# One fused attention and mixture kernel: the three row buffers become a ring of twelve 512-column pieces

## The reference

```python
h = _layernorm(x) * (1 + ca) + sa
q, k, v = linear(h) ; scores = q @ k.T / sqrt(128)
qp = linear(h, Wtq)                     # two coordinates per token
diff = qp[i] - qp[j]
dist_sq = sum(diff ** 2)
forward_bias = 0.5 * (1 + cos(atan2(diff_y, diff_x)))
valid = (dist_sq <= mean + 1.25 * std) & causal
weights = softmax(where(valid * forward_bias == 0, -inf, scores))
x = x + ga * (h + linear(weights @ v) + 0.1 * linear(qp / norm(qp)))
h = _layernorm(x) * (1 + cb) + sb
x = x + gb * mixture(h)   # top 4 of 16 experts by routing, and 2 shared ones
```

## Time and profile before

| what | us |
|---|---|
| median of 3 runs | 665.44 |
| lowest and highest | 664.79, 666.22 |
| the profiled execution, its own time | 664.28 |
| span of the profiled execution | 662.5 |
| TensorE busy | 568.8 |
| VectorE busy | 512.1 |
| ScalarE busy | 362.5 |
| GpSimd busy | 362.1 |

### The profile page before, as it was taken

One profiled execution on the slowest core, in us unless ns is written; L12 is line 12 of the kernel. 1 busy time (PEld: TensorE's weight loads), 2 busy tenths in 40 slices (PEclk: granted clock), 3 DMA queues, 4 the chain that ended last, 5 costly groups with the idle time before them and its releaser, 6 DMA issues.

```text
span 662.5 us, 10953 instructions
## 1 busy us (share of the span) xinstructions
PE 568.8 (86%) x3524; PEld 342.4 (52%) x3524; DVE 512.1 (77%) x1448; ACT 362.5 (55%) x722; POOL 362.1 (55%) x325
## 2 busy tenths in 40 slices
PE   2846878887877899898989999799988599999995
PEld 1734445565653454354545555465554365656563
DVE  3588899997776688656776675756976999898887
ACT  0623567687642633356775868655455355555552
POOL 4459455844104452869977677733314355555553
PEclk9997679898987799899998999999999999999999
DMA  6501000000004121131112220122100000000000
GB/s 187 159 2 35 1 0 1 1 0 1 1 13 115 69 72 45 63 96 49 63 48 60 69 65 32 51 63 63 49 1 16 2 1 17 2 17 2 17 1 17
DMA packets 21840, 26.01 MB, mean 39 GB/s; under 512 B 2628, under 2 KB 11864, under 8 KB 21784
## 3 DMA queue, kind: packets, MB, share of 16 engines
q1 hardware_dynamic: 21784, 25.33, 13.1%
HBM read 23.09 MB, written 2.23 MB: 38 GB/s over the span
## 4 chain that ended last, share of the span: by engine, by line
PE 42%; DVE 34%; issue 8%; ACT 7%; POOL 6%; SPq 1%; DMA 1%; DVEq 0%; ACTq 0%; POOLq 0%
PE bank L805 7%; PE bank L1053 7%; PE bank L806 7%; PE bank L807 6%; DVE row L1322 4%; PE bank L954 4%; DVE stage L1536 4%; ACT stage L745 4%; DVE pen L1328 3%; DVE row L1333 3%; DVE ysb L1515 2%; PE bank L939 2%; POOL sw L580 2%; PE bank L844 2%; PE bank L914 2%
## 5 line engine op out<-in xcount | busy, mean ns | idle before, releaser
L594 POOL TENSOR_TENSOR gp<-stage,gp 128x512 f16<-128x512 f32 x72 | 83.6, 1161 | 73.6 <-ACT gp L762 73.6
L580 POOL TENSOR_TENSOR sw<-hid,gp 128x512 f32<-128x512 f32 x64 | 81.4, 1271 | 76.9 <-DVE hid L1462 70.4
L1462 DVE SCALAR_TENSOR_TENSOR hid<-stage,bank 128x512 f32<-128x512 f32 x72 | 49.2, 684 | 63.5 <-ACT stage L745 62.1
L745 ACT ACTIVATE stage<-bank 128x512 f32<-128x512 f32 x144 | 84.7, 588 | 22.9 <-PE bank L807 22.6
L762 ACT CAST gp<-stage 128x512 f16<-128x512 f32 x72 | 44.4, 617 | 72.8 <-DVE stage L1536 72.8
L538 POOL TENSOR_TENSOR row<-row,dx 128x512 f32<-128x512 f32 (+3 forms) x48 | 54.6, 1141 | 54.3 <-ACT dx L642 54.0
L699 ACT COPY ptr<-bank 128x512 f32<-128x512 f32 (+2 forms) x80 | 41.5, 518 | 78.2 <-PE bank L939 77.6
L1053 PE MATMUL bank<-stage,wd 128*128 128x512 f32 x144 | 76.7, 615 | 7.2 <-DVE ysb L1467 7.2
L954 PE MATMUL bank<-v,ptr 128*128 128x128 f32 x544 | 77.0, 283 | 3.3 <-DVE x L1308 3.3
L954 PEld LDWEIGHTS bank<-v,ptr 128*128 128x128 f32 x544 | 70.9, 200 | 5.3 <-issue 3.9
L1515 DVE SCALAR_TENSOR_TENSOR ysb<-bank,comb,ysb 128x128 f32<-128x128 f32 x240 | 67.1, 342 | 0.1
(11 more groups left out here) (256 smaller groups left out, 1315.9 us busy)
## 6 DMA issues: line engine op xcount, KB each, us to landing
gp<-shares SPq DMA_DIRECT2D x64, 256.0 KB, 3.1
out_x<-x SPq DMA_DIRECT2D x8, 256.0 KB, 2.3
stage<-in_L_ffn_gate_w SPq DMA_DIRECT2D x1, 576.0 KB, 7.5
stage<-in_L_ffn_up_w SPq DMA_DIRECT2D x1, 576.0 KB, 4.2
stage<-in_L_ffn_gate_w SPq DMA_DIRECT2D x1, 448.0 KB, 6.9
stage<-in_L_ffn_up_w SPq DMA_DIRECT2D x1, 448.0 KB, 3.6
row<-in_L_wmod SPq DMA_DIRECT2D x1, 384.0 KB
stage<-in_L_ffn_sh_gate_w SPq DMA_DIRECT2D x1, 128.0 KB, 5.6
```

The costliest lines, as they stand in the source:

```text
L580: pool.tensor_tensor(sw[:, s % 2, :], hid[:, s % 2, :], wb[:, n % HELD_WEIGHTS, :], ALU.mult)\
L594: pool.tensor_tensor(gp[:, n % HELD, 1, :], act_g[:, s % 2, :], gp[:, n % HELD, 0, :], ALU.subtract)\
L745: act.activation(sg[:, s % 2, :], gate_bank(s)[:, :], func, scale=half_of / (H_UP * W_UP))\
```

## The change

`row` keeps its size but is now read as a ring of 12 pieces of 512 columns; chunk m lies in piece m % 12. The table `MEASURES_AT` is gone. In every slot n, ScalarE makes the rise of chunk n + 6, and GpSimd its measure where GpSimd has that chunk. In input piece 24, ahead of slot 0, six chunks are made in place of two. The wait of a rise is now for the turning of chunk m - 12. Masking, exponential and transposes address the new place; their sizes and counts are the same.

```diff
-ROWS = 3
+UNITS = 12
+AHEAD = 6
...
-RISE_AT = {CHUNKS_BEFORE[i - ROWS + 1] + CHUNKS_ROW[i - ROWS]: i for i in range(ROWS, BLK)}
-
-MEASURES_AT = {0: [2]}
-for slot, i in RISE_AT.items():
-    for c in range(CHUNKS_ROW[i]):
-        MEASURES_AT.setdefault(slot + c, []).append(CHUNKS_BEFORE[i] + c)
...
+        def unit_of(m):
+
+            k, o = divmod(m % UNITS, CH)
+            return row[:, k, o * W:(o + 1) * W]
...
@@ gpsimd, input piece 24 and the slots
                 if k == PIECES - 1 and b:
-                    for m in range(2):
+                    for m in range(AHEAD):
                         measure(b, m)
...
-                for m in MEASURES_AT.get(n, ()):
-                    if by_pool(b, m):
-                        measure(b, m)
+                if n + AHEAD < NCH and by_pool(b, n + AHEAD):
+                    measure(b, n + AHEAD)
...
@@ scalar, rise
-                if i >= ROWS:
-
-                    act.wait_ge(probs_turned, NCH * b + CHUNKS_BEFORE[i - ROWS] + min(c + 1, CHUNKS_ROW[i - ROWS]))
-                act.activation(row[:, i % ROWS, lot], yb[:, lot], ACT.Abs, bias=nyi[:, i:i + 1]).then_inc(rise_ready, 1)
+                if m >= UNITS:
+
+                    act.wait_ge(probs_turned, NCH * b + m - UNITS + 1)
+                act.activation(unit_of(m)[:, 0:w], yb[:, lot], ACT.Abs, bias=nyi[:, i:i + 1]).then_inc(rise_ready, 1)
...
@@ scalar, input piece 24 and the slots
-                    for m in range(2):
+                    for m in range(AHEAD):
                         rise(b, m)
...
-                for m in MEASURES_AT.get(n, ()):
-                    rise(b, m)
+                if n + AHEAD < NCH:
+                    rise(b, n + AHEAD)
```

More of the change, by code:

```diff
@@ L181, in build @@
         pen = sb("pen", [P, 2, W], BF16); dx = sb("dx", [P, 2, W])
-        row = sb("row", [P, ROWS, N])
+        row = sb("row", [P, 3, N])
         gsgn, gmag, graw = (row[:, 0, k * W:(k + 1) * W] for k in range(3))
@@ L536, in measure @@
                 pool.wait_ge(dx_ready, pooled(b, m))
-                o = row[:, i % ROWS, c * W:c * W + w]
+                o = unit_of(m)[:, 0:w]
                 pool.tensor_tensor(o, o, dx[:, pooled(b, m) % 2, 0:w], ALU.subtract).then_inc(measure_ready, 1)
@@ L702, in attention @@
                     i, c = CHUNKS[m]
-                    lot = slice(c * W, min((c + 1) * W, (i + 1) * P))
+                    probs = unit_of(m)[:, 0:min(W, (i + 1) * P - c * W)]
                     act.wait_ge(max_ready, BLK * b + i + 1)
-                    act.activation(row[:, i % ROWS, lot], row[:, i % ROWS, lot], ACT.Exp, bias=nmx[:, i:i + 1],
+                    act.activation(probs, probs, ACT.Exp, bias=nmx[:, i:i + 1],
                                    accum_out=rsum[:, i, c:c + 1]).then_inc(probs_ready, 1)
-                for m in MEASURES_AT.get(n, ()):
-                    rise(b, m)
+                if n + AHEAD < NCH:
+                    rise(b, n + AHEAD)
                 if n in NORM_AT:
@@ L939, in attention @@
                         last = pe.transpose(ring(b, 2, m)[:, k * P:(k + 1) * P],
-                                            row[:, i % ROWS, j * P:(j + 1) * P], ident[:, :])
+                                            unit_of(m)[:, k * P:(k + 1) * P], ident[:, :])
                     last.then_inc(probs_turned, 1)
@@ L1314, in attention @@
                     L = (i + 1) * P
-                    o = row[:, i % ROWS, :]
+                    w = min(W, L - c * W)
+                    o = unit_of(n)
                     if by_pool(b, n):
@@ L1321, in attention @@
                         dve.wait_ge(rise_ready, NCH * b + n + 1)
-                        step(dve.scalar_tensor_tensor(out=o[:, lot], in0=xb[:, lot], scalar=nxi[:, i:i + 1],
-                                                      in1=o[:, lot], op0=ALU.add, op1=ALU.subtract, reverse1=True))
+                        step(dve.scalar_tensor_tensor(out=o[:, 0:w], in0=xb[:, lot], scalar=nxi[:, i:i + 1],
+                                                      in1=o[:, 0:w], op0=ALU.add, op1=ALU.subtract, reverse1=True))
                         settle()
-                    w = min(W, L - c * W)
                     dve.wait_ge(dist_made, NCH * b + n + 1)
                     dve.scalar_tensor_tensor(out=pen[:, n % 2, 0:w], in0=ring(b, 1, n)[:, 0:w], scalar=0.0,
-                                             in1=o[:, c * W:c * W + w], op0=ALU.min, op1=ALU.min)\
+                                             in1=o[:, 0:w], op0=ALU.min, op1=ALU.min)\
                        .then_inc(dist_used, 1)
@@ L1332, in attention @@
                     dve.wait_ge(scores_made, NCH * b + n + 1)
-                    dve.tensor_tensor_reduce(o[:, c * W:c * W + w], ring(b, 0, n)[:, 0:w], pen[:, n % 2, 0:w],
+                    dve.tensor_tensor_reduce(o[:, 0:w], ring(b, 0, n)[:, 0:w], pen[:, n % 2, 0:w],
                                              float(P) ** -0.5 / QK_UP ** 2, -3.0e38, ALU.add, ALU.max,
```

## The result

The changed kernel takes 669.09 us (median of 16 runs, 667.17 to 672.61), the kernel before 666.15 in 16 runs beside it (664.38 to 668.24). The ratio is 1.005, with a 95% interval of 1.0036 to 1.0064: 3.3 us slower by the ratio, while the two medians are 2.9 apart. The profiled execution took 668.51 us with a span of 666.7, 4.2 more than the 662.5 of before. 6.0 us were predicted.

The account below looks back on a forecast made before the run. Bound by VectorE in batch 0; in batch 1 by ScalarE's chain at step 25, then GpSimd, then TensorE. 4.9 + 1.1 - 0.8 + 0.8 = +6.0 us on the median 665.44 gives 671.4, range 668.4 to 673.8.

Parts of the forecast that it names:

- The new wait: In every slot, a rise of chunk m waits for the turning of chunk m - 12; claimed to add 0.
- Six pairs ahead of step 25: Batch 1, input piece 24: ScalarE does chunks 2 to 5 before step 25's activation, on the path; +4.9 us (4.4 to 5.3).
- GpSimd's stretch: Batch 1, from step 25's `weigh` to the layer norm's power: heavier measures on gapless GpSimd; +1.1 us (0 to 1.5).
- The clock behind the new stall: Batch 1, behind step 25's gate product: TensorE's clock falls, but GpSimd paces the next 32 us; 0.
- rival 2: Behind step 25's stall TensorE's clock falls and TensorE has no room: 1.7 us lost, +7.7 in all, 673.1; chance 0.08.
- Slot 12: Batch 1: chunk 14's 128-wide pair leaves ScalarE's path ahead of the down product; -0.8 us (bounds 0 to -2.5).
- rival 3: Evenness pays: doubled slots of batch 1 each return a pair and a clock fall, 2.5 us; -0.7, 664.7; chance 0.04.
- slot 12 alone: Batch 1: only slot 12's gap becomes short enough for TensorE's clock to stay up; +4.3 us in all, 669.7.
- Batch 0: Slots 27 to 31: GpSimd's earlier measures and residual pieces lengthen VectorE's subtraction L1322; +0.8 us (0 to +1.8).
- Slots 14 to 39: Batch 1: doubled slots 14, 24, 27 and added pairs in 17, 31 cost 0; TensorE hides ScalarE in 14 to 27.
- The refund (rival 1): Batch 1, slots 8 to 12, paced by GpSimd or ScalarE, return 1.85 us, not 0.8; +4.95, 670.4; chance 0.12.

Follow-up runs that it names:

- experiment 1: The changed kernel with batch 1's first six rise pairs and measures spread over input pieces 21 to 24; ratio 1.0005 to the kernel before.
- experiment 6: The changed kernel with GpSimd's power for the layer norm ahead of its slot's measure, not behind it; ratio 1.0036 to the kernel before.
- Experiment 4: The changed kernel with one more 128-wide pair of ScalarE operations in batch 1's slot 12, written to an unread buffer; ratio 1.0101 to the kernel before.
- Experiment 8: The changed kernel with a lead of 4 chunks in batch 0 and still 6 in batch 1; ratio 1.0061 to the kernel before.

## Why the prediction was right, and which terms were off

The direction, the place and the largest term were right: 669.09 is inside the range of 668.4 to 673.8, near its lower end. The 6.0 us forecast are 3.3 by the ratio, and 4.2 by the profile. That the number is inside has some luck in it: the forecast was added to a median of 665.44, and the kernel before took 666.15 beside the changed one. From 665.44 the measured 3.3 us give 668.7, inside by 0.3. What held the range open that far down was the bound of -2.5 at slot 12, the very term that came out there.

- *The new wait, 0:* right. No rise waited for a turning.
- *Six pairs ahead of step 25, +4.9:* 4.85 by the trace; experiment 1 takes it back (4.4). The sum of the four pitches was exact, since ScalarE does the pairs back to back.
- *GpSimd's stretch, +1.1:* 1.06. GpSimd is gapless, and experiment 1, without the burst, shows the same 1.06. What the term leaves out is that TensorE's own work stands some 0.5 us behind (experiment 6).
- *The clock behind the new stall, 0 (rival 2 had 1.7):* right. The clock fell to 0.50 and GpSimd covered it.
- *Slot 12, -0.8:* the failed size. The pair was 0.78, but behind the gap of 1.98 us the clock stayed up, and 1.6 more came back. I had this as the tail of rival 3 ("slot 12 alone, +4.3") and as the bound of -2.5, and took the pair alone. Experiment 4, which puts 0.6 us of gap back and loses 2.2, shows it, in one profile; that the five profiles with a gap of 1.98 us all kept the clock speaks for it. But the trace of before also had a gap of 2.93 us, in front of 482.57, with the clock at 1.00 behind it, so the length alone could not have foretold it. Rival 3 itself falls: in slots 14 to 27 nothing moved (4.06 to 4.06).
- *Batch 0, +0.8:* wrong in sign. It was -0.2 by the profile (0.48 at slot 26 to 0.26 at slot 39). I took half a GpSimd instruction for each meeting from rows in which L1322 came second; where it came first, GpSimd stood still, and had the time. Experiment 8 bears it out for a lead of 4. The prediction named batch 0's slots ending earlier as a sign of being wrong; counted from slot 26 they did, and this term is what was wrong.
- *Slots 14 to 39, 0:* +0.2.
- *The refund (rival 1):* it had 1.85 us come back by slots 8 to 12, as pairs. What came back was 2.4, at the chunk's end alone, and by the clock.

With -2.4 in place of -0.8, -0.2 in place of +0.8 and +0.2 in place of 0 for slots 14 to 39 the sum is 3.5 us (4.85 + 1.06 - 2.4 - 0.2 + 0.2), beside 3.3 by the ratio, with 2.4 to 4.3 as its interval; the profile's 4.2 has 0.5 of late start and 0.3 between the batches besides. (Two thirds of the way down from 671.4 is 668.7, where the prediction has 668.6; nothing hangs on it.)

## What to carry to other kernels

Making work earlier is not free where it is all made at one place: ask what stands behind the burst on each in-order engine, and add up its pitches. Fill the lead from steps in which the engine idles, and leave the steps empty that feed a chunk's end. And where TensorE stands still, look at its granted clock behind the gap, in more than one execution: a gap that is a little shorter was worth three times here what it was shortened by, and a gap of unchanged length cost 1.7 us in one execution and nothing in another.

## What the runs showed of the hardware

- A small difference of a gap can decide on the clock, and the length alone does not: in the eleven profiles, behind the down product's gaps at the two chunk ends of batch 1's slots, TensorE's granted clock over the next 4 us was 0.57 to 0.71 in fourteen (gaps of 2.20 to 3.62 us) and 1.00 in eight (1.34 to 1.98). But behind the gap of 2.92 or 2.93 us that follows the last mask it was 1.00 in seven and 0.50 to 0.68 in four, and the four lost 1.7 to 3.0 us. What else decides is not shown here.
- Where VectorE's L1322 (two SBUF inputs) and GpSimd meet, the one that begins second is stretched: L1322 from 0.74 to 2.86 us, or GpSimd's 128x512 subtraction from 1.27 to 1.73 and its L525 from 1.04 to 1.38. How far is regular: a 128-partition, 512-column L1322 that begins inside a GpSimd instruction takes what is left of that instruction plus 0.55 us, or 0.74 where that is less. In the trace of before 0.84 us were left at 145.97 (1.39 taken) and 2.31 at 99.21 (2.86); all 121 that begin so in the eleven profiles agree within 0.02. GpSimd's two were longer by 0.1 us less than what was left of L1322 (0.48 left and 0.34 longer, 0.58 and 0.46).
- The clock also differs where the code doesn't: its mean from 154 to 166 us in batch 0 is 0.86 in eight profiles and 0.72 to 0.74 in three, with up to 1.7 us between them by the end of batch 0's slots, and from 182 to 230 us it is 0.79 to 0.89, with up to 3.9 us. This, and a start that varies by up to 3 us, is why single profiles of these kernels differ by more than their edits.
